# Splitting the batch of a field-pair interaction kernel into chunks of 256, 512, 512, 512 and 256 rows in place of 128, 384, 512, 512 and 512

## What is computed

```python
e = jnp.stack([tbl_f[ids[:, f]] for f in range(32)], axis=1)       # (2048, 32, 64)
rows, cols = np.triu_indices(32, k=1)                              # 496 pairs of fields
p, q = e[:, rows, :], e[:, cols, :]
pij = jnp.einsum('bpe,dpe,bpd->bp', p, kernel, q)                  # a 64x64 form for each pair
z = pij @ W.T + b                                                  # (2048, 256)
h = jnp.concatenate([z, dense_ctx], axis=1)                        # (2048, 272)
h = jnp.maximum(h @ W_top1 + b_top1, 0.0)                          # (2048, 512)
h = jnp.maximum(h @ W_top2 + b_top2, 0.0)                          # (2048, 256)
y = h @ W_top3                                                     # (2048, 1)
```

## Time and profile before

| what | us |
|---|---|
| median of 3 runs | 882.09 |
| lowest and highest run | 881.82, 883.49 |
| the profiled execution's own time | 880.07 |
| its span, in which all times of the trace lie | 878.1 |
| TensorE busy (PE) | 838.8 (96%) |
| VectorE busy (DVE) | 632.9 (72%) |
| GpSimd busy (POOL), gathers | 483.9 (55%) |
| ScalarE busy (ACT) | 71.7 (8%) |

### The profile page before, as it was taken

How to read it: one execution, slowest core, us unless ns; L and a number is a source line. 1 busy time by engine, 2 the same in 40 slices (tenths; PEclk the granted TensorE clock), 3 DMA queues, 4 the chain that set the end, 5 groups by cost and what they waited for, 6 DMA issues and landing times.

```text
span 878.1 us, 33839 instructions
## 1 busy us (share of the span) xinstructions
PE 838.8 (96%) x15748; PEld 346.6 (39%) x15748; DVE 632.9 (72%) x694; ACT 71.7 (8%) x136; POOL 483.9 (55%) x517
## 2 busy tenths in 40 slices
PE   5767899999999999999999999999999999999988
PEld 3545545444443333333333333333333333333333
DVE  3556676799986558999885548999875557999950
ACT  0000011100011110000011110000011111000001
POOL 6777777777777777777777777777720000000000
PEclk9899999999999999999999999999999999999999
DMA  9511111111111111111111111111100000000000
GB/s 333 185 31 30 32 29 30 30 29 31 28 30 28 28 29 28 29 28 29 29 29 29 27 28 29 29 30 28 29 13 2 1 1 2 2 3 2 2 3 0
DMA packets 21597, 29.36 MB, mean 33 GB/s; under 512 B 11121, under 2 KB 11665, under 8 KB 20945
## 3 DMA queue, kind: packets, MB, share of 16 engines
q0 software_dynamic: 16384, 16.81, 10.4%
q1 hardware_dynamic: 3394, 8.79, 2.7%
q10 hardware_dynamic: 1680, 1.61, 0.6%
HBM read 27.17 MB, written 0.01 MB: 31 GB/s over the span
## 4 chain that ended last, share of the span: by engine, by line
PE 94%; issue 3%; DVE 2%; DMA 1%; ACT 0%; SPq 0%; ACTq 0%; DVEq 0%
PE bilinear L448 52%; PE sums L468 26%; PE bilinear L494 11%; PE bilinear L431 4%; DVE w_comb_sb L368 1%; DMA b_sb<-b_top 1%; DVE prod L387 1%; PE bilinear L406 0%; PE bilinear L401 0%; SPq L261 0%; DMA sums_sb<-dense_t 0%; ACTq L298 0%; DVE prod L384 0%; DVE prod L382 0%; DVEq L180 0%
## 5 line engine op out<-in xcount | busy, mean ns | idle before, releaser
L387 DVE TENSOR_TENSOR prod<-bilinear,emb_t 128x1024 f32<-128x1024 f32 (+2 forms) x600 | 579.4, 1006 | 192.5 <-PE bilinear L448 185.3
L280 POOL DMA_INDIRECT emb<-table,ids_sb x512 | 483.4, 944 | 158.7 <-issue 155.3
L448 PE MATMUL bilinear<-emb_t,k_sb 64*32 64x512 f32 (+2 forms) x10240 | 523.2, 507 | 14.1 <-issue 12.0
L448 PEld LDWEIGHTS bilinear<-emb_t,k_sb 64*32 64x32 f32 x10240 | 190.2, 107 | 281.2 <-issue 250.7
L468 PE MATMUL sums<-prod,row_sel 64*32 64x512 f32 (+2 forms) x4960 | 286.6, 508 | 7.7 <-issue 7.3
L468 PEld LDWEIGHTS sums<-prod,row_sel 64*32 64x32 f32 x4960 | 88.7, 107 | 118.1 <-issue 83.0
L316 ACT ACTIVATE emb_t<-bilinear 128x512 f32<-128x512 f32 (+2 forms) x80 | 40.8, 513 | 501.5 <-PE bilinear L431 463.1
L494 PE MATMUL bilinear<-sums_sb,w_comb_sb 128*128 128x512 f32 (+2 forms) x160 | 59.8, 519 | 3.4 <-DMA sums_sb<-dense_t 1.5
L431 PEld LDWEIGHTS bilinear<-ident,emb 128*128 128x128 f32 x256 | 27.3, 141 | 53.2 <-DVE prod L387 47.8
L431 PE MATMUL bilinear<-ident,emb 128*128 128x128 f32 x256 | 45.4, 291 | 1.8 <-DVE w_comb_sb L368 1.6
L494 PEld LDWEIGHTS bilinear<-sums_sb,w_comb_sb 128*128 128x128 f32 x160 | 27.1, 190 | 36.8 <-issue 25.5
(11 more groups left out here) (12 smaller groups left out, 12.2 us busy)
## 6 DMA issues: line engine op xcount, KB each, us to landing
emb<-table,ids_sb POOLq DMA_INDIRECT x512
k_sb<-k_slots SPq DMA_DIRECT2D x2, 1088.0 KB, 11.5
k_sb<-k_slots SPq DMA_DIRECT2D x1, 1600.0 KB
k_sb<-k_slots SPq DMA_DIRECT2D x1, 1472.0 KB, 15.0
k_sb<-k_slots SPq DMA_DIRECT2D x1, 960.0 KB, 9.2
k_sb<-k_slots SPq DMA_DIRECT2D x1, 896.0 KB, 20.7
k_sb<-k_slots SPq DMA_DIRECT2D x1, 576.0 KB, 10.4
h_sb<-w_cols ACTq DMA_DIRECT2D x1, 512.0 KB, 4.0
```

The costliest lines, as they stand in the source:

```text
L280: nc.gpsimd.indirect_dma_start(emb[:, j, t, f % 2, :], None, tables[f], bass.IndirectOffsetOnAxis(ap=ids_sb[:, start + t, f:f + 1].bitcast ...
L387: last = nc.vector.tensor_tensor(prod[:, at:at + 2, 0:n], bilinear[:, bank:bank + 2, 0:n], emb_t[:, j:j + 1, 0:n].to_broadcast([P, 2, n]), ...
L448: last = nc.tensor.matmul(bilinear[col:col + QUARTER, bank + row // EMB, 0:n], k_sb[row:row + EMB, s, col:col + QUARTER], emb_t[row:row + ...
```

## The change

Only the table of chunk sizes changes. The new file has one more empty line above it, so every line of the kernel below stands one further down (L280 becomes L281).

```diff
-CHUNK_TILES = (1, 3, 4, 4, 4)
+
+CHUNK_TILES = (2, 4, 4, 4, 2)
```

## The result

The changed kernel takes **896.33 us** (median of 4 runs, 894.74 to 898.29), the kernel before 881.96 beside it. The ratio is 1.0163, 95% interval 1.0145 to 1.018: 1.6% slower, where the forecast was 890.8, 1.0% slower, with a range of 884 to 899. The profiled execution took 896.29, its span is 893.7 (before: 880.07 and 878.1), where the forecast had a span of 886.8.

The account below looks back on a forecast made before the run. TensorE bounds the kernel now; after the change, GpSimd's gathers bind in chunk 1. Span 246.0 + 535.7 + 199.8 - 1.5 - 83.7 - 11.5 + 2.0 = 886.8; profiled execution 888.8, median 2.0 above: 890.8 us, range 884 to 899.

Parts of the forecast that it names:

- The new wait: Chunk 1: TensorE waits for gathers at each turn from about 127 us; double 15, ready about 200, turned at 246; 82%.
- the first rival: Chunk 1: gathers below 1.0 us each keep up, chunk 1 ends at 310 not 352, kernel about 848 us; 5%.
- The half clock ahead of the gathers: Rival, chunk 1: half-clock work of 11.2 us per 10.0 us double, double 15 at worst 8 us late, 899 us; 7%.
- the clock term: Behind chunk 1's double 15: half clock after idling costs at most 3.4 us, taken as 2.0; covered by gather waits before.
- the end: After the last chunk's sums: copies, dense context and layers at half width, 18.6 us for 30.1, so -11.5.
- Chunk 4: Narrow last chunk, 256 rows for 512: 115.9 us for 199.6, so -83.7; bounds 112.2 to 119.
- the 3.6 us for a block: Chunk 4: each 256 instructions take 3.6 us against TensorE's 3.43, adding 2.9 us over 46 phases without layers.
- the 199.8 for the chunk that moved: Behind chunk 1's double 15: one 512-row chunk more than behind chunk 2's double 15 today, +199.8 us.
- Signs of the view: After trace: TensorE's busy share falls some 4 points; GpSimd may pause a little for chunk 3's turns.
- the two margins here, 9 and 17 us: Kernel before: gathers land 9 us ahead of chunk 1's last turn, 17 ahead of chunk 2's double 15; the change spends these.

Follow-up runs that it names:

- g1: Changed kernel with GpSimd gathering only two of four tiles of each chunk 1 double, plain SyncE loads of fixed table rows replacing the others; 855.8 us.
- g4: Changed kernel with slots, products and quads of chunk 4 using 128 of 256 columns, as many instructions; 1313.42 us, in a session with TensorE held back early.
- e3: Changed kernel with VectorE multiplying only 128 of the 256 columns of chunk 4's slots; 1318.17 us, in a session with TensorE held back early.
- h1: Changed kernel with chunks of 2, 3, 4, 4, 3 tiles and chunk 1's turns placed late; 859.11 us undisturbed, ratio 0.9741 to the kernel before.

## Why the prediction was right, and where it was off

*The new wait.* Right, in place and time, and the cause is shown by g1. Double 15 of chunk 1 was said to be turned at 246.0 and its copy began at 246.07. That TensorE would be ready at about 200 was some 9 us too hopeful: g1 has the copy at 208.88. Hence the price of the wait is 37 us, not the 42 (310 against 352) that the first rival's working gives. The 122 at which chunk 0 was to be done is 126.9 in the trace, in part since twelve turns of its own were left there and not eight; as the prediction said, with the gathers in the lead that costs nothing.

*The first rival, gathers that keep up.* Its mechanism didn't take place: gathers stayed 1.25 us apart, again. In g1, where fewer gathers do the same for it, its sign is right and its time, 848, is 8 too low.

*The half clock ahead of the gathers.* The clock fell in chunk 1 as the clock term said it could, and never got ahead of the gathers. Of five such stretches, the first and the last; then two slices that hold the second, the end's, and what follows that, for TensorE alone:

```profile
134.80:141.70 6.90, 6.14 (x66) 0.51 0.14 27
233.80:240.60 6.80, 5.24 (x44) 0.50 0.12 24
...
154.10:157.50 3.40, 1.96 (x7) 0.68 0.14 29
157.50:160.90 3.40, 3.40 (x38) 0.82 0.13 27
...
875.50:882.30 6.80, 6.10 (x14) 0.50 0.00 0
882.30:893.70 11.40, 7.95 (x35) 1.00 0.00 1
```

The first and the last are 6.8 us long; the second, by 0.32 and 0.18 of full clock missing in two slices of 3.4 us, is 3.4 us long, and so are the third and the fourth. The last cost TensorE some 2.6 us of work (half of its busy 5.24), and it still stood 1.56 us before the turn of double 15. The wait of 37 us is 28.7 us of idle time (25.0 + 2.0 + 1.7) and the rest slower work in its cover (TensorE is busy for 92.2 us up to double 15, and for 83.9 in g1), which is why the waits' own total, 25.0, understates the cost. The Trainium skill, "TensorE: Matmul & The Clock Gate", section "HAM oscillation — how this bites in real kernels", describes a fall in each wait for a DMA, so that the work behind it starts at the low clock. By this trace the falls come, though not in each (five for the eleven waits), and cost nothing as long as the other side sets the time. Where I put the term, behind double 15, it was zero: the clock was back at 240.6. It belonged to the end, where TensorE idles for the dense context (2.1 us before 876.2) and a half clock has nothing to hide under: 21.6 us, and 18.6 in g1, which idles as long and keeps the full clock. Nothing in the trace before tells which of the two an execution gets. That is the first of the two mis-sized terms: **2.0 at the wrong place, where 3.0 were due at another**.

*Chunk 4.* The second: **115.9 forecast, 120.8 measured**, outside the bounds of 112.2 to 119 that the prediction gives it. Half of today's chunk without the layers of chunk 3 is 112.2; of the 8.6 above that, 3.7 lie in the last 40 phases (56.5 for half of 105.7), where I had about 3. So the 3.6 us for a block were nearly right (3.7), and so was their cause, by g4 and e3: instruction fetch, with VectorE's share small. The miss is in the first 24 phases, to which I gave next to nothing: 64.3 for 59.4. Turns of two tiles come 5.68 us apart (copies at 744.88 and 750.56) where four-tile ones are 5.90, so a turn costs 0.53 rather than half of 0.74, 1.9 us for twelve; and two quads of the first phases belong to chunk 3 and are 512 wide still, 0.9 us. The four such turns in chunk 3 are nearly all of its 0.7 as well (the forecast took off 1.5, and by 0.53 it is 0.8). About 2 us there stay unexplained. To halve a row of the table one must ask which of its instructions belong to this chunk, and which of them have a fixed part.

On instruction fetch the Trainium skill ("Runtime: NRT & Kernel Launch", "Instruction fetch mechanics") says "mostly hidden". At 512 and 384 columns this trace agrees; at 256 and 128 it doesn't, and g4's stretch of 56.4 us for 36.8 us of work is the clearest sight of it.

*The sum, and luck in it.* The span was 6.9 us too low, the time only 5.5: I had added 2.0 because the median before lay that much above its profiled execution, and of the changed kernel it doesn't (896.33 and 896.29). The 2.0 for a clock fall that had no effect where I put it covers part of the 3.0 at the end in the same way. The wait itself, the 199.8 for the chunk that moved and the time of double 15 are no luck; that two mis-sized terms stayed within the range is in part.

*Signs of the view.* TensorE's share fell by 2 points, not 4: chunk 0 has 7.9 us of idle time, and had 21.6, and the matmuls at half clock count as busy. GpSimd paused for chunk 3's turns, 9.8 us in all, unseen at the end.

## What to carry to other kernels

An engine that nobody waits for is a bound in waiting: take its rate, count its instructions up to each point where its product is asked for, and compare with when that point comes; the two margins here, 9 and 17 us, decided the sign of a change that would have saved some 27 us without the wait (g1). Where such a wait appears, look first at when the product is asked for and when it is used, before the amount of work; h1 speaks for it, but the turns alone, with nothing else moved, were not measured undisturbed. And a chunk gets hardly cheaper below the width at which its instructions are worked off as fast as they come: here 40 phases take 56.4 us at 128 columns and 56.5 at 256.

## What the runs showed that I had not expected

TensorE was held to one matmul every 2.8 us until about 130 us in three of five sessions, in every kernel traced there. The comparison with the kernel before comes out otherwise there. The 2, 4, 4, 4, 2 sizes with late turns reach 0.963 to 0.969 of it, and 2, 3, 4, 4, 3 only 0.988 to 0.992, where undisturbed the latter has 0.974. The changed kernel itself was not run there, but e3 is that kernel with at most some 2 us taken out of chunk 4, and takes 1318.17 us beside 1372. So by this one execution what is 1.6% slower undisturbed is some 4% faster there, and late turns bring it nothing (1324.49). What holds TensorE back no run here shows.

What a half clock costs depends on who sets the time: some 24 us of it in chunk 1 (a granted 0.90 over 119.2 us) moved double 15 by nothing, 6.8 us at the end cost 1.9 (384 columns) and 3.0 (256), by executions of the same layers with and without it.
